# Two norms in a row in the second layer's attention: one stage with two roots in place of two stages

## The reference

```python
def _layernorm(x, axis=-1, eps=1e-05):
    m = jnp.mean(x, axis=axis, keepdims=True)
    v = jnp.var(x, axis=axis, keepdims=True)
    return (x - m) / jnp.sqrt(v + eps)
...
    x = x + _L1_attn_ref(_layernorm(x, axis=-1), L1_attn_qK, L1_attn_qV, ...)
    x = x + _L1_ffn_ref(_layernorm(x, axis=-1), L1_ffn_Wg, ...)
```

```python
def _L1_attn_ref(x, qK, qV, kK, kV, vK, vV, pK, pV, fK, fV):
    ...
    x_in = x
    h = layer_norm(x)
    k = pattention(h, kK, kV)
    q = pattention(h, qK, qV)
    v = pattention(h, vK, vV)
    ...
    o = pattention(o, pK, pV)
    x = o + x_in
    x_inter = x
    x = pattention(layer_norm(x), fK, fV)
    return x + x_inter
```

## Time and profile before

| | us |
|---|---|
| median of 3 runs | 3994.05 (3987.98 to 4000.08) |
| profiled execution | 3999.98 |
| its span | 3998.1 |
| PE / DVE / ACT / POOL busy | 3313.5 / 2547.3 / 1793.1 / 1220.8 |
| mean granted clock of PE | 0.891 |

### The profile page before, as it was taken

One profiled execution on the slowest core, in us unless ns is written; L12 is line 12 of the kernel. 1 busy time (PEld: TensorE's weight loads), 2 busy tenths in 40 slices (PEclk: granted clock), 3 DMA queues, 4 the chain that ended last, 5 costly groups with the idle time before them and its releaser, 6 DMA issues. The chain is left out here.

```text
span 3998.1 us, 44732 instructions
## 1 busy us (share of the span) xinstructions
PE 3313.5 (83%) x12501; PEld 1548.3 (39%) x12573; DVE 2547.3 (64%) x4074; ACT 1793.1 (45%) x2808; POOL 1220.8 (31%) x1036
## 2 busy tenths in 40 slices
PE   5499996999997598867897788888878788489998
PEld 2122225444444254434544233333333254454443
DVE  6888864433346576745433699999999853545444
ACT  2066661444435255533332676776776422212121
POOL 3211110000002222210000699999999800210000
PEclk7699996999997699978798888999899979789999
DMA  3222200000001432110000333333333210000000
GB/s 101 63 72 62 61 28 26 0 0 0 0 27 45 117 98 86 55 34 0 1 0 23 125 143 138 145 143 136 144 148 138 95 40 3 0 0 0 0 0 21
DMA packets 112299, 232.33 MB, mean 58 GB/s; under 512 B 27461, under 2 KB 82138, under 8 KB 94618
## 3 DMA queue, kind: packets, MB, share of 16 engines
q1 hardware_dynamic: 108026, 228.54, 17.0%
q0 software_dynamic: 4096, 1.59, 0.2%
HBM read 191.98 MB, written 34.87 MB: 57 GB/s over the span
## 5 line engine op out<-in xcount | busy, mean ns | idle before, releaser
L1103 DVE TENSOR_REDUCE a_top<-a_sc 128x1 f32<-128x512 f32 (+3 forms) x1024 | 545.2, 585 | 175.8 <-PE a_sc L980 105.3
L2033 DVE TENSOR_TENSOR_SCAN a_g<-a_decay,a_drive 128x512 f32<-128x512 f32 x512 | 588.1, 1202 | 32.6 <-ACT a_drive L1953 32.3
L2096 POOL TENSOR_TENSOR a_g<-a_g,a_spread 128x1024 f32<-128x1024 f32 x256 | 599.6, 2360 | 27.8 <-DVE a_g L2033 27.7
L1061 ACT ACTIVATE a_prob<-a_st 128x1024 f32<-128x1024 f32 (+2 forms) x512 | 419.3, 862 | 323.9 <-PE a_st L997 206.8
L571 DVE TENSOR_TENSOR f_s<-f_a,f_spread 128x512 f32<-128x512 f32 x392 | 269.5, 688 | 441.3 <-PE f_spread L429 193.7
L1813 PE MATMUL a_y<-a_g,ident 128*128 128x512 f32 x1024 | 498.0, 628 | 55.1 <-POOL a_g L2096 51.2
L402 PE MATMUL f_hid<-h,f_w 128*128 128x512 f32 x784 | 407.8, 602 | 0.6 <-DVE h L493 0.6
L411 PE MATMUL f_y<-f_s,f_w 128*128 128x512 f32 x784 | 402.9, 596 | 4.5 <-DVE x L581 3.6
L977 PE MATMUL a_sc<-a_k,a_q 96*128 96x512 bf16 (+3 forms) x1024 | 309.0, 357 | 34.7 <-DMA a_k<-a_k_rows 32.5
L1813 PEld LDWEIGHTS a_y<-a_g,ident 128*128 128x128 f32 x1024 | 202.6, 203 | 344.0 <-issue 248.5
L1937 ACT ACTIVATE a_decay<-a_delta,a_capped_a 128x512 f32<-128x512 f32 x512 | 331.7, 709 | 6.5 <-DVE a_g L2033 5.9
(11 more groups left out here) (362 smaller groups left out, 5077.2 us busy)
## 6 DMA issues: line engine op xcount, KB each, us to landing
a_spread<-a_bc_rows SPq DMA_DIRECT2D x128, 1024.0 KB, 4.6
a_q<-a_q_rows SPq DMA_DIRECT2D x192, 96.0 KB
a_pv_rows<-a_pv_sb SPq DMA_DIRECT2D x64, 256.0 KB, 2.1
a_k<-a_k_rows SPq DMA_DIRECT2D x288, 32.0 KB
a_k<-a_k_rows SPq DMA_DIRECT2D x288, 16.0 KB
a_num<-a_pv_rows SPq DMA_DIRECT2D x16, 256.0 KB, 3.6
a_q_rows<-p_qp SPq DMA_DIRECT2D x24, 128.0 KB
a_q_rows<-a1q_qp SPq DMA_DIRECT2D x24, 128.0 KB
```

The costliest lines, as they stand in the source:

```text
L1061: nc.scalar.activation(prob[w % 2][:, j, 0:width(kp)], st[:, j % 2, 0:width(kp)], ACT.Exp, scale=a.scale).then_inc(s.exp_done, 1)
L1103: nc.vector.tensor_reduce(top[:, t, n:n + 1], sc[:, slot(4 * n + t) % 3, 0:w], AX.X, ALU.max).then_inc(s.maxed, 1)
L2033: nc.vector.tensor_tensor_scan(g[:, n % 8, k, way], decay[:, n % 4, k, way], drive[:, k, way], 0.0, ALU.mult, ALU.add).then_inc(scanned, 1)
L2096: nc.gpsimd.tensor_tensor(g[:, n % 8, :, :], g[:, n % 8, :, :], spread[:, pair % 4, 2 + n % 2:3 + n % 2, :].to_broadcast([P, H2, L]), ALU. ...
```

## The change

A new function `layer_norm_twice` takes the place of both calls. Means, centring, squares and variances are done once. ACT then takes two roots of the same `var`, sqrt(v+e) and sqrt(v(1+e)+e*e), DVE refines both reciprocals in one chain of 128x64, PE turns the parts of both (two bf16 matmuls in place of one in f32), and for each chunk eight matmuls spread both rows into two banks of the four. DVE makes two products a chunk, `twice` (g) and `once` (h, in place). A chunk's pair of banks is written again when the chunk two before has been multiplied. The loops are written out, and the attention's 10 loads are put ahead of the feed-forward's in the one stage. All other stages are as they were.

```diff
--- before.py
+++ after.py
@@ -237,6 +237,134 @@
                 nc.gpsimd.memset(buf[:, :], 0.0).then_inc(S.cleared, 1)
             if call == 0:
                 build_selectors(nc, S, pool)
+def layer_norm_twice(nc, S, src, once, twice):
+    call = S.ln_calls
+    S.ln_calls += 1
+    pending, primes = S.pending, S.primes
+    S.pending, S.primes = [], []
+    clears, S.clears = S.clears, []
+    S.n_cleared += len(clears)
+    n_cleared = S.n_cleared
+    base = NB * call
+    eps_set = S.sem(f"ln2_eps{call}")
+    with ExitStack() as ctx:
+        def sb(name, shape, dt=F32):
+            return ctx.enter_context(nc.sbuf_tensor(f"ln2_{name}{call}", shape, dt))
+        sq = [sb(f"sq{k}", [P, L]) for k in range(2)]
+        eps = sb("eps", [P, 1])
+        parts, rows = sb("parts", [P, 2, 96], BF16), sb("rows", [96, 2, P], BF16)
+        part, rest = sb("part", [P, 2, NT], BF16), sb("rest", [P, 2, NT])
+        std, v, rstd = sb("std", [P, 2, NT]), sb("v", [P, 2, NT]), sb("rstd", [P, 2, NT])
+        ring = ctx.enter_context(nc.psum_tensor(f"ln2_ring{call}", [P, 4, L], F32))
+        var = ctx.enter_context(nc.psum_tensor(f"ln2_var{call}", [P, NT], F32))
+        turned = ctx.enter_context(nc.psum_tensor(f"ln2_turned{call}", [96, 2, P], F32))
+        block = ctx.enter_context(nc.Block())
+        if pending:
+            @block.sync
+            def _(sp):
+                if clears:
+                    sp.wait_ge(S.cleared, n_cleared)
+                for to, what, sem in pending:
+                    sp.dma_start(to, what).then_inc(sem, 16)
+        @block.tensor
+        def _(pe):
+            def means(c):
+                pe.wait_ge(S.ln_centered, base + c + 1)
+                nc.tensor.matmul(ring[:, c % 4, :], S.mean_w[:, :], src[:, chunk(c)],
+                                 start=True, stop=True).then_inc(S.ln_mean, 1)
+            def variances(c):
+                pe.wait_ge(S.ln_squared, base + c + 1)
+                for t in range(TC):
+                    last = nc.tensor.matmul(var[:, c * TC + t:c * TC + t + 1], sq[c % 2][:, t * P:(t + 1) * P],
+                                            S.mean_w[:, 0:1], start=True, stop=True)
+                last.then_inc(S.ln_var, 1)
+            for c in range(4):
+                means(c)
+            for i in range(NB // 2):
+                variances(2 * i)
+                variances(2 * i + 1)
+                if 2 * i + 4 < NB:
+                    means(2 * i + 4)
+                    means(2 * i + 5)
+            pe.wait_ge(S.ln_rstd, call + 1)
+            pe.wait_ge(S.setup_step, 6)
+            for j in range(2):
+                last = nc.tensor.matmul(turned[:, j, :], parts[:, j, :], S.ident_b[:, :], start=True, stop=True)
+            last.then_inc(S.ln_turned, 1)
+            pe.wait_ge(S.ln_rows, call + 1)
+            pe.wait_ge(S.ln_centered, base + NB + 4)
+            for c in range(NB):
+                if c >= 2:
+                    pe.wait_ge(S.ln_normed, base + 4 + c - 1)
+                for j in range(2):
+                    for t in range(TC):
+                        last = nc.tensor.matmul(ring[:, 2 * (c % 2) + j, t * P:(t + 1) * P], S.sel[:, c * TC + t, :],
+                                                rows[:, j, :], start=True, stop=True)
+                last.then_inc(S.ln_spread, 1)
+        @block.vector
+        def _(dve):
+            for sem, count in primes:
+                dve.sem_inc(sem, count)
+            nc.vector.memset(eps[:, :], EPS * EPS).then_inc(eps_set, 1)
+            for c in range(NB):
+                dve.wait_ge(S.ln_mean, base + c + 1)
+                nc.vector.tensor_tensor(once[:, chunk(c)], src[:, chunk(c)], ring[:, c % 4, :],
+                                        ALU.subtract).then_inc(S.ln_centered, 1)
+            dve.wait_ge(S.ln_std, call + 1)
+            chain = Chain(dve, S.ln_step, 8 * call)
+            nc.vector.tensor_scalar(v[:, 0, :], var[:, :], EPS, None, ALU.add)
+            nc.vector.tensor_scalar(v[:, 1, :], var[:, :], 1.0 + EPS, EPS * EPS, ALU.mult, ALU.add)
+            chain(nc.vector.reciprocal(rstd[:, :, :], std[:, :, :]))
+            chain(nc.vector.tensor_tensor(v[:, :, :], v[:, :, :], rstd[:, :, :], ALU.mult))
+            chain(nc.vector.tensor_tensor(v[:, :, :], v[:, :, :], rstd[:, :, :], ALU.mult))
+            chain(nc.vector.tensor_scalar(v[:, :, :], v[:, :, :], -0.5, 1.5, ALU.mult, ALU.add))
+            chain(nc.vector.tensor_tensor(rstd[:, :, :], rstd[:, :, :], v[:, :, :], ALU.mult))
+            chain(nc.vector.tensor_copy(part[:, :, :], rstd[:, :, :]))
+            nc.vector.tensor_copy(parts[:, :, 0:NT], part[:, :, :])
+            chain(nc.vector.tensor_tensor(rest[:, :, :], rstd[:, :, :], part[:, :, :], ALU.subtract))
+            chain(nc.vector.tensor_copy(part[:, :, :], rest[:, :, :]))
+            nc.vector.tensor_copy(parts[:, :, SELW:SELW + NT], part[:, :, :])
+            nc.vector.tensor_tensor(parts[:, :, 2 * SELW:2 * SELW + NT], rest[:, :, :], part[:, :, :],
+                                    ALU.subtract).then_inc(S.ln_rstd, 1)
+            dve.wait_ge(S.ln_turned, call + 1)
+            nc.vector.tensor_copy(rows[:, :, :], turned[:, :, :]).then_inc(S.ln_rows, 1)
+            for c in range(NB):
+                dve.wait_ge(S.ln_spread, base + c + 1)
+                nc.vector.tensor_tensor(twice[:, chunk(c)], once[:, chunk(c)], ring[:, 2 * (c % 2) + 1, :], ALU.mult)
+                nc.vector.tensor_tensor(once[:, chunk(c)], once[:, chunk(c)], ring[:, 2 * (c % 2), :],
+                                        ALU.mult).then_inc(S.ln_normed, 1)
+        @block.scalar
+        def _(act):
+            for c in range(NB):
+                act.wait_ge(S.ln_centered, base + c + 5)
+                act.wait_ge(S.ln_var, base + c + 1)
+                nc.scalar.activation(sq[c % 2][:, :], once[:, chunk(c)], ACT.Square).then_inc(S.ln_squared, 1)
+            act.wait_ge(S.ln_var, base + NB + 2)
+            act.wait_ge(eps_set, 1)
+            nc.scalar.activation(std[:, 0, :], var[:, :], ACT.Sqrt, bias=S.eps[:, 0:1])
+            nc.scalar.activation(std[:, 1, :], var[:, :], ACT.Sqrt, bias=eps[:, 0:1], scale=1.0 + EPS
+                                 ).then_inc(S.ln_std, 1)
+        @block.gpsimd
+        def _(pool):
+            for buf in clears:
+                nc.gpsimd.memset(buf[:, :], 0.0).then_inc(S.cleared, 1)
 def mixture(nc, S, f):
@@ -1656,9 +1784,9 @@
                  (values[:, 0, :], inp["L1_attn_qV"]), (values[:, 1, :], inp["L1_attn_kV"]),
                  (values[:, 2, :], inp["L1_attn_vV"]), (pkeys[:, :], inp["a1_pKT"]), (pvalues[:, :], inp["L1_attn_pV"]),
                  (fkeys[:, :], inp["a1_fKT"]), (fvalues[:, :, :], inp["L1_attn_fV"].rearrange("(n p) c -> p n c", p=P))]
-        S.pending += [(dst, src, s.loaded) for dst, src in loads]
+        S.pending = [(dst, src, s.loaded) for dst, src in loads] + S.pending
         s.loaded_count = 16 * len(loads)
-        layer_norm(nc, S, S.h, g)
+        layer_norm_twice(nc, S, S.x, S.h, g)
         pattention(nc, S, "a1q", g, keys[:, :], [values[:, n, :] for n in range(3)], [1, 1, 1], a=a)
         attend(nc, S, a)
         combine(nc, S, a, g)
@@ -2559,7 +2687,6 @@
             fs["f1"] = mixture_1(S, inp, sb_middle)
             S.primes += fs["f1"].primes
         if "a1" in stages:
-            layer_norm(nc, S, S.x, S.h)
             layer1_attention(nc, S, inp)
         if "f1" in stages:
             mixture(nc, S, fs["f1"])
```

## The result

| | before | after |
|---|---|---|
| median of the runs | 3994.52 us (4 runs, 3987.98 to 4000.08) | 3960.69 us (4 runs, 3956.09 to 3963.44) |
| profiled execution | 3999.98 us, span 3998.1 | 3959.54 us, span 3957.6 |
| mean granted clock | 0.891 | 0.896 |

What follows compares the result with a forecast made beforehand. The two norms were taken as serial chains without overlap, PE then DVE bounding them. Removing 26.22 us and adding 6.84 gives net -19.4: 3974.7 us from a median of 3994.05, range 3963 to 3986 or 3987.

Steps and rivals of the forecast that it cites:

- The merged stage: The one norm stage replacing two: 24.08 us plus 6.84 added, 30.9 us in all.
- The second root: ACT's extra root in the merged stage: 0.2 us added, bounds 0.03 and 0.29.
- the reciprocal: DVE's reciprocal on 64 columns in place of 32, at 6.4 ns a column: 0.20 us added, about 0.54 in all.
- the rows' copy: Copy of 256 columns out of PSUM in place of 128: 0.13 us added.
- the turn: On PE, two bf16 matmuls for one f32 of 0.45 us: no difference, within 0.15 us either way.
- 12.0 us from the first load to the end: Spreading on PE and 16 products on DVE, eight chunks: 12.0 us where it was 6.01, 5.97 added.
- The ring: Reuse of a pair of PSUM banks between PE and DVE: one round 2.68 us, 1.34 a chunk.
- The first (the clock rises): PE reaches 2.4 GHz during the spreading, so products and first scores run faster: 3973.2 us, chance 0.12.
- The second (one pair of banks at a time): PE takes up a chunk only after the pair just before: 2.68 us a chunk, 9.4 more, 3984.1 us, chance 0.04.
- The third (a lower clock later): Attention after the norms runs at 0.78 mean clock, not 0.87: 45.6 us more, 4020 us, chance 0.03.
- every us taken from the stretch is a us of the end, unless a later stage runs otherwise: The two norms' stretch overlaps no neighbouring stage, so its net 19.4 us saving reaches the kernel's end.
- 0.01 of mean clock: Allowance in the range for the attention behind the norms: 4.5 us either way.

Runs made afterwards that it cites:

- before_written_out: Kernel before with the loops of layer 1's two norms written out, nothing merged: 3985.95 us (10 runs), ratio 0.9975.
- the runs with fillers: Kernel before with 2 to 256 empty semaphore increments on PE at the head of layer 1's `attend`; with 8: 3988.46 us, with 115: 3983.64 us.
- n = 141: Changed kernel with 141 empty semaphore increments on PE at the head of layer 1's `attend`: 3971.18 us (5 runs).

## Why the prediction was wrong

**The merged stage: right, and 1.3 us too dear.** The second root came 0.19 us behind the first (0.2 forecast), the reciprocal took 0.54 us (as worked out from 6.4 ns a column), the rows' copy 0.42 and the turn 0.45. The one mis-sized term is "12.0 us from the first load to the end", which took 10.79. Its two inputs came from a loop with a register for the chunk: 0.90 us from load to first product, and 0.631 a product. Written out, the products come every (1194.64 - 1185.60) / 15 = 0.603 us, and the first one 1.07 us after the first spreading with eight loads where I had 1.31; before_written_out shows both savings (0.597 and 0.25 us) without any merge. The ring then goes round in 1.28 + 0.06 + 1.07 = 2.41 us, 1.20 a chunk, which is DVE's own pace, so it costs nothing: PE idles only 0.16 to 0.19 us a chunk.

**The rivals.** The first (the clock rises) didn't come: 0.50 in both windows of the spreading. The rule of the Trainium skill (TensorE: Matmul & The Clock Gate, "What's actually happening"), that sustained activity releases the clock, did not bring the level up within this stretch, with PE busy 3.13 and 3.49 of 4 us and a pause behind each chunk. The second (one pair of banks at a time) is refuted by 1.20 us a chunk. The third (a lower clock later) went the other way: 0.88 over the 510 us behind the stage, against 0.87.

**The step that failed** is "every us taken from the stretch is a us of the end, unless a later stage runs otherwise", with a range that let the later stages differ only by 0.01 of mean clock. They ran otherwise, by a mechanism that I did not look for: PE stops at the back edges of layer 1's attention, and for how long depends on what stands ahead of the loop in PE's stream. The edit shortens that stream, and with that moves the head of the loop against the blocks in which instructions are fetched. In the kernel before, the runs with fillers show that the place decides; for the changed kernel it is concluded from there, as its second stops are gone in every trace but the one try to bring them back (n = 141) failed. Two turns of the loop took

| back edges | builds | two turns, mean (range), us |
|---|---|---|
| with a second stop | 5 | 177.6 (175.9 to 179.0) |
| without | 11 | 169.0 (167.1 to 174.6) |
| none | 4 | 162.9 (161.4 to 165.5) |

so the second stops cost 8.6 us (10.7 by the two unchanged and the three changed traces alone). The gaps themselves are 6.6 of it (13.3 us in sum against 6.6), and the low clock behind them can hold the rest. The rows had this before the change: two idle times of 7 us with "issue" as their cause stood in PE's timeline of `attend`, and I only read that stage's total.

**The account.** Over three sets the change gives 30.7 us in the mean: 20.7 in the merged stage, 8.6 at the back edges, and 1.4 that I can't tell from the scatter. Of the two profiled executions, 40.5 us apart: 20.7, then 179.0 - 167.7 = 11.3 in the two turns, 4.6 in the opening (85.0 against 80.4), 3 at 1850 to 1945, and 0.9 elsewhere. With the back edges' 8.6 put back, the three medians of the changed kernel, 3965.1 in the mean, would be 3973.7, where 3974.7 was forecast.

**What stays open.** Why the opening of the attention takes 78 to 92 us in the traces of kernels before (72 and 64 with 115 and 256 fillers, which delay its start on PE) and 80 to 87 in those of kernels after, with waits for the maxima's rows of 7 to 17 us in sum (0.7 with 256 fillers); it varies between executions of one kernel (85.0 and 78.4). And whether the changed kernel could be made slow by the right number of fillers: the one try (n = 141) did not do it. And whether one chunk a turn in place of two, half the body, would keep the loop in PE's memory and its back edges at 0.2 us; it wasn't tried.

**The fastest version** is the changed kernel with `attend` written out: 3956.87 and 3963.3 us in two sets. It beats the kernel before in both; from the changed kernel's 3960.7, 3970.4 and 3964.1 it can't be told apart with certainty, though its two turns are 6 us shorter.

## What to carry to other kernels

Before you price an edit in a long program with loops, look in the timeline for idle time with "issue" as its cause behind each engine's back edges: it depends on where the loop's head lies, so any edit ahead of it can take it away or bring it. A forecast of a small effect needs a line in its range for that, here 9 us on 20; to measure an edit alone, write the loop out in both versions and run the pair in one set. And take paces from written-out code when the new code is written out: 0.03 us an instruction and 0.25 us ahead of the first product went with the loop.

## What the runs showed of the hardware

- The same PE loop pays 0.2 us a back edge with a body of 1317 instructions and no instruction transfer in its turn, and 3.4 to 5.2 us of branch with a body of 1831 and nine or more transfers. By the two turns' length a back edge of the second kind is (169.0 - 162.9) / 2 = 3 us, and (177.6 - 162.9) / 2 = 7.4 us with a second stop.
- Eight empty instructions made the kernel 8.2 us faster (ratio 0.998, 0.997 to 0.999).
- After a stop of 7 us PE worked at a mean clock of 0.70 over 10 us without idle time; after stops of 3 to 4 us the windows show 1.00 at the changed kernel's first back edge and 0.83 at its second.
- DVE, ACT and POOL have the same loop in `attend`, and their branches took 0.04 to 0.08 us: only PE, with the longest body, paid.
- Two roots of 128x32 on ACT start 0.19 us apart, though one takes 0.29.
